# Cross-attention plus mixture-of-experts block: the second layer of the last pair but one in two parts, other buffers and another order of fetches behind the pairs

## The reference

```
x = x + tanh(g_xattn[0]) * xattn(layernorm(x), ctx)      # 16 heads of 64, 64 context rows
x = x + tanh(g_ffn[0])   * ffn(layernorm(x))
ffn:   shared = (sum over 2 shared experts of gelu(x @ sw1 + sb1) @ sw2 + sb2) / 2
       gates  = x @ router_w + router_b;  top 2 of 8 experts, softmax over the two
       moe    = sum over the two chosen of prob * (gelu(x @ w1[e] + b1[e]) @ w2[e] + b2[e])
       return shared + moe
```

## Time and profile before

| what | us |
|---|---|
| three runs: median (lowest to highest) | 379.96 (378.42 to 380.06) |
| the profiled execution's own time | 378.79 |
| span of its trace | 377.1 |
| PE busy | 368.1 |
| DVE busy | 280.7 |
| ACT busy | 239.9 |
| POOL busy | 219.8 |

### The profile page before, as it was taken

The page is one execution under the profiler, slowest core; times in us unless marked ns, Lnnn a source line. Parts: engine busy times, 40 slices in busy tenths (PEclk is TensorE's granted clock), DMA queues, the critical chain, the costliest instruction groups (busy, mean ns, idle before and its releaser), DMA issues.

```text
span 377.1 us, 8869 instructions
## 1 busy us (share of the span) xinstructions
PE 368.1 (98%) x2805; PEld 349.8 (93%) x2806; DVE 280.7 (74%) x612; ACT 239.9 (64%) x538; POOL 219.8 (58%) x268
## 2 busy tenths in 40 slices
PE   8999999999999999999999999999999998999996
PEld 7987989999999899899999989999999997889995
DVE  5799898888988997799899887555655554554486
ACT  2675456556656635787878857666666665677740
POOL 6558775788788762477782245556565654653200
PEclk9999999999999999999999999999999999999999
DMA  7990000000000066502930112213222324650397
GB/s 219 292 350 20 2 30 15 16 27 30 14 14 28 17 241 248 237 4 35 303 115 3 29 44 86 72 56 95 75 87 81 93 79 127 199 138 29 108 352 253
DMA packets 33855, 40.15 MB, mean 106 GB/s; under 512 B 9690, under 2 KB 26524, under 8 KB 33692
## 3 DMA queue, kind: packets, MB, share of 16 engines
q1 hardware_dynamic: 28976, 29.40, 25.3%
q0 software_dynamic: 4768, 10.28, 8.9%
q10 hardware_dynamic: 76, 0.02, 0.0%
HBM read 27.88 MB, written 11.68 MB: 105 GB/s over the span
## 4 chain that ended last, share of the span: by engine, by line
PE 79%; DMA 6%; DVE 5%; issue 3%; ACT 3%; POOL 3%; DVEq 0%; ACTq 0%; POOLq 0%
PE psum L1385 11%; PE psum L1362 11%; PE psum L1278 10%; PE psum L1322 10%; PE psum L1619 8%; PE psum L1525 7%; PE psum L1499 5%; PE psum L1580 4%; DMA y_rows<-ybuf 4%; PE psum L1238 3%; DMA xsl<-y_rows,table 2%; PE psum L1512 1%; PE psum L1604 1%; PE psum L1136 1%; PE psum L1310 1%
## 5 line engine op out<-in xcount | busy, mean ns | idle before, releaser
L762 POOL DMA_INDIRECT y_tok<-ysl,table x39 | 38.9, 997 | 42.0 <-ACT ysl L1047 37.1
L755 POOL DMA_INDIRECT xsl<-y_rows,table x39 | 39.3, 1008 | 32.1 <-PE psum L1385 11.8
L728 POOL DMA_INDIRECT names<-named,pos x32 | 35.2, 1099 | 12.8 <-issue 8.2
L683 POOL TENSOR_TENSOR Eb<-Eb,rinv 128x512 f32<-128x512 f32 x32 | 33.5, 1065 | 11.6 <-DVE rinv L1833 11.6
L1091 ACT ACTIVATE hr<-psum,b_cur 128x256 f32<-128x256 f32 x48 | 20.1, 471 | 22.1 <-DVE b_cur L2128 12.3
L924 ACT ACTIVATE yTb<-psum 128x256 f32<-128x256 f32 x16 | 6.2, 384 | 42.6 <-PE psum L1342 42.6
L1619 PE MATMUL psum<-xsT_hi,w_cur 128*128 128x256 f32 x192 | 31.0, 284 | 0.0
L663 POOL TENSOR_TENSOR half_sum<-Eb 128x512 f32<-128x512 f32 x16 | 20.7, 1292 | 11.5 <-ACT Eb L879 11.3
L2177 DVE TENSOR_TENSOR hr_lo<-hr,hr_hi 128x512 fp32r<-128x512 f32 x24 | 16.6, 693 | 13.3 <-ACT hr_hi L1104 13.0
L1619 PEld LDWEIGHTS psum<-xsT_hi,w_cur 128*128 128x128 f32 x192 | 26.5, 192 | 0.0
L1047 ACT ACTIVATE ysl<-psum,table 128x256 f32<-128x256 f32 x39 | 17.1, 466 | 12.8 <-PE psum L1499 8.7
(11 more groups left out here) (275 smaller groups left out, 1247.6 us busy)
## 6 DMA issues: line engine op xcount, KB each, us to landing
w_raw<-in_L_ffn_w SPq DMA_DIRECT2D x2, 4096.0 KB, 16.8
y_got<-y_tok SPq DMA_DIRECT2D x8, 512.0 KB, 7.6
sw_raw<-in_L_ffn_sw SPq DMA_DIRECT2D x2, 1024.0 KB, 12.3
y_rows<-ybuf SPq DMA_DIRECT2D x16, 128.0 KB, 1.7
sw_lo_kept<-sw_lo SPq DMA_DIRECT2D x1, 2048.0 KB, 8.7
sw_lo<-sw_lo_kept SPq DMA_DIRECT2D x8, 256.0 KB, 3.5
xs_all<-in_x SPq DMA_DIRECT2D x3, 512.0 KB, 13.8
out<-xs_all SPq DMA_DIRECT2D x3, 512.0 KB, 3.1
```

The lines of the kernel that those rows point to most:

```text
L683: nc.gpsimd.tensor_tensor(Eb[q][:, heads, :], Eb[q][:, heads, :], rinv[:, q, heads].unsqueeze(2).broadcast_to([P, H // 2, CTX]), ALU.mult) ...
L728: nc.gpsimd.indirect_dma_start(names, bass.IndirectOffsetOnAxis(ap=pos[:, k, t:t + 1], axis=0), named[:, k, t, :], None).then_inc(scattere ...
L755: nc.gpsimd.indirect_dma_start(into[:, s % 2, :], None, y_rows, bass.IndirectOffsetOnAxis(ap=table[:, s, 0:1].bitcast(I32), axis=0)).then_ ...
L762: nc.gpsimd.indirect_dma_start(y_tok, bass.IndirectOffsetOnAxis(ap=table[:, s, 1:2].bitcast(I32), axis=0), ysl[:, s % 2, :], None).then_in ...
```

## The change

- PE: the second layer of 26/27 is made in two parts, h = 0 in `double(11)` where all of it stood, h = 1 in `step(30)` behind the transposes of 31.
- Tile 30's rows are gathered into `xsl2` instead of `xsl`; the waits of gathers 30 to 32 and of the later transposes are renumbered to fit.
- POOL: gather 31 moves from d = 9 (behind gather 30) to d = 10 (behind scatters 24 and 25, ahead of gather 32). Gather 34 moves ahead of scatter 28. The order is now: scatter 22, 23, gather 30; scatter 24, 25, gather 31, 32; scatter 26, 27; gather 33, 34; scatter 28, 29; gather 35; scatter 30; gather 36 and so on.
- ACT, in d = 11: the high part of tile 31's rows is taken ahead of `kept(1)`.
- DVE: `half_left(1)` of the pair 28/29 moves into `step(30)`, behind the low part of tile 31's rows; `bias_weights` moves from d = 10 to `step(33)`, behind `hidden_left(32)`.

```diff
@@ gather
-                elif 1 <= d < DOUBLES:
+                elif 1 <= d < DOUBLES or s == SINGLE1:
                     pool.wait_ge(xt_psum, s - 3)
+                elif SINGLE1 < s < SINGLE1 + 3:
+                    pool.wait_ge(xt_psum, SINGLE1)
                 elif s >= 2:
                     pool.wait_ge(xt_psum, s - 1)
-                into, loaded = (xsl3, xsl2_loaded) if d == 0 else (xsl2, xsl2_loaded) if wide(d) else (xsl, xsl_loaded)
+                second = wide(d) or s == SINGLE1
+                into, loaded = (xsl3, xsl2_loaded) if d == 0 else (xsl2, xsl2_loaded) if second else (xsl, xsl_loaded)
@@ POOL's order
-                    if d + 3 == DOUBLES:
-                        gather(SINGLE1 + n)
+                if d + 3 == DOUBLES:
+                    gather(SINGLE1)
                 if d + 2 == DOUBLES:
+                    gather(SINGLE1 + 1)
                     gather(SINGLE1 + 2)
-            for s in range(SINGLE1 + 1, SLOT_TILES):
-                if s + 2 < SLOT_TILES:
-                    gather(s + 2)
+            gather(SINGLE1 + 3)
+            gather(SINGLE1 + 4)
+            scatter(SINGLE1 - 2)
+            for s in range(SINGLE1 + 2, SLOT_TILES):
                 scatter(s - 3)
+                if s + 3 < SLOT_TILES:
+                    gather(s + 3)
@@ ACT, double
-                kept(1)
                 if d == DOUBLES - 1:
                     turned(SINGLE1 + 1, 1)
+                kept(1)
@@ PE, turn
-                pe.wait_ge(xsl_loaded[par], 16 * (s // 2 + 1) if s < DOUBLE0 else 16 * (s // 2 + 1) - 16 * (DOUBLES // 2))
+                rows = xsl2 if s == SINGLE1 else xsl
+                if s == SINGLE1:
+                    pe.wait_ge(xsl2_loaded[0], 16 * (DOUBLES // 2 + 1))
+                elif s < DOUBLE0:
+                    pe.wait_ge(xsl_loaded[par], 16 * (s // 2 + 1))
+                else:
+                    pe.wait_ge(xsl_loaded[par], 16 * ((s + par) // 2 - DOUBLES // 2))
@@ PE, give_wide, step, double
-            def give_wide(s, n):
+            def give_wide(s, n, halves=range(2)):
...
-                for h in range(2):
+                for h in halves:
...
-                if s == SINGLE1 + 1:
+                if s == SINGLE1:
+                    give_wide(s - 4, 0, range(1, 2))
+                elif s == SINGLE1 + 1:
                     give_wide(s - 3, 1)
-                elif s >= 2 and s != SINGLE1:
+                elif s >= 2:
...
-                    give_wide(s - 2, 0)
+                    give_wide(s - 2, 0, range(1))
@@ DVE, step, double (half_left now takes the tile as well)
-                if s >= 1 and s != SINGLE1:
+                if s == SINGLE1:
+                    half_left(s - 2, 1)
+                elif s >= 1:
                     hidden_left(s - 1, 1 - par)
+                if s == SINGLE1 + 3:
+                    bias_weights(EARLY, LAST)
...
                 if d == DOUBLES - 1:
                     bias_and_hidden(SINGLE1, 0)
-                half_left(1)
+                else:
+                    half_left(s, 1)
                 if more:
                     move_weights(par, 1)
-                if d == DOUBLES - 2:
-                    bias_weights(EARLY, LAST)
```

More of the change, by code:

```diff
@@ L1487, in turn @@
                 for k in range(KD):
-                    last = nc.tensor.transpose(bank[par][:, k * P:(k + 1) * P], xsl[:, par, k * P:(k + 1) * P], ident[:, :])
+                    last = nc.tensor.transpose(bank[par][:, k * P:(k + 1) * P], rows[:, par, k * P:(k + 1) * P], ident[:, :])
                 last.then_inc(xt_psum, 1)
@@ L2170, in step, with half_left @@
                     columns_rest(EARLY, late)
+            def half_left(s, h):
+                dve.wait_ge(ht_hi, s + (h + 1))
+                nc.vector.tensor_tensor(hr2_lo[:, 2 * h:2 * h + 2, :], hr2[:, :, :], hr2_hi[:, 2 * h:2 * h + 2, :].bitcast(F32),
+                                        ALU.subtract).then_inc(ht_lo, 1)
             def double(d, par, s, j):
[L2174 to L2178, removed]
                 if d == 0:
@@ L2191, in double @@
                     turned_wide(s + 2, 1 - par)
-                half_left(0)
+                half_left(s, 0)
                 if more:
```

## The result

The changed kernel took 380.65 us (median of 11 runs, 379.71 to 381.96), the kernel before 379.02 us in the same session (11 runs, 377.73 to 380.06). The ratio is 1.0038 with a 95% interval of 1.0023 to 1.0053, that is 1.4 us slower (0.9 to 2.0). The forecast was 380.2 us, 0.7 above its base, with its likeliest case inside 0.5%.

The account below looks back on a forecast made before the run. PE, busy for 98% of the span, was taken as the bound. The terms 0.50 + 1.07 - 1.01 + 0.15 = +0.7 us on a base of 379.5 gave 380.2 us, range 378.2 to 382.2.

Parts of the forecast that it names:

- its base: Starting time of 379.5 us, set between the profiled execution's 378.79 and the three-run median 379.96.
- its likeliest case: Whole kernel: +0.7 us, giving 380.2 us, chance 0.57; no change was given 0.71.
- the deciding step: POOL fetching tile 31's rows one place later: PE stops from 313.06 to 314.94, first layer 31 +0.50 us.
- Halves of the second layer: PE, second layer 26/27 in two parts: 12 products take 1.44 us, first layer 30 starts about 311.68 instead of 313.26.
- The 0 for tile 30's low part: Before first layer 30: PE's wait for the low part of tile 30's rows, taken as 0, upper end 0.3 us.
- Gather 31: POOL slot at 312.10, landing 2.8 us, rows at 314.90; first layer 31 at 317.12 instead of 316.62, +0.50 us.
- Outputs and scatter 27, up to first layer 33: ACT and POOL: output 26 2.05 later, scatter 27 landing in 3.8, gelu 31 at 323.9; first layer 33 +1.07 us.
- Step 34: PE's wait for gather 35, landing at 331.1 with transposes due at 331.55, is gone: -1.01 us.
- `bias_weights` in step 33: DVE: 1.72 us of work delays `hs` of 34 to about 333.1; +0.15 us, bounds 0 and 1.0.
- Sum: Whole kernel: 0.50 + 1.07 - 1.01 + 0.15 = +0.7 us, put on 379.5 to give 380.2 us.
- the first term: Wait for tile 31's rows before first layer 31: +0.50 us; +0.3 with a 2.6 us landing, +1.5 with 3.8.
- "from both sides": Gather 30 on POOL keeps its place, more than 4 us before it is due: 0 either way.

## Why the prediction was right

The sign, the size within 1 us, and the deciding step held; one cause was overlooked and one small term missed. By the prediction's steps:

- *Halves of the second layer.* First layer 30 was to start 4.62 us behind first layer 28/29 (311.68); it did at 4.72, since the 12 products took 1.60 us (310.61 to 312.21) instead of 1.44. The 0 for tile 30's low part was right: gelu started at 310.14, where 311.39 was before.
- *Gather 31.* Slot expected at 312.10, which is 312.53 on the changed trace's clock; it was 312.45. Landing 2.8 taken, 3.1 measured, idle time 1.88 taken, 1.81 measured. First layer 31 came 0.74 later than before (10.30 against 9.56) instead of 0.50: the 0.3 of the landing. That this place on POOL decides is shown by putting it back: -2.7 us.
- *Outputs and scatter 27, up to first layer 33.* +1.07 expected, +0.89 measured (1.63 less the 0.74). Output 26 was to be 2.05 later and was 2.30 later, counted from first layer 28/29; scatter 27 landed in 3.6 (3.8 taken), and gelu 31 started at 324.37, the predicted 323.9 plus the 0.43 by which this trace runs late. But PE's recorded wait in that step is for gather 33, which I had listed as standing in the queue and never given a landing time: issued at 321.57, there at 324.8. The two waits end within 0.1 us of each other, so the size was right for a reason that was only half of it, and that is luck. The kernel with gather 33 early shows scatter 27's half by itself (0.51 us of idle time); with gather 33 early and the reload late neither is left, and step 32 takes 3.48 us.
- *Step 33.* I had no term for scatter 28's landing and output 30. It cost 0.41 us (3.89 instead of 3.48).
- *Step 34.* -1.01 expected, 3.50 instead of 4.49 measured: -0.99. Gather 35 took 3.8 us, not the 5.1 taken, but PE asked for it 1.8 us behind its landing, so this did not matter.
- *`bias_weights` in step 33.* +0.15 taken, 0.02 measured; `hs` of 34 was done at 333.78 and its transposes started at 334.12. In exchange the move is what lets the halves work at all, which the prediction used (gelu at 309.9) but did not price: 1.4 us, by the two kernels that differ in it with gather 31 early (0.9967 and 1.0003).
- *Sum.* +0.7 predicted, +1.05 in the trace (26.99 against 25.94), +1.4 (0.9 to 2.0) over the runs. The base of 379.5 was 0.5 above the 379.02 measured for the kernel before, which made up for about half of what the sum lacked: between the medians the change cost 1.6 us, and 380.2 lies 0.45 below the 380.65 measured. That 380.2 came so close is in part luck.

The prediction's sentence that gathers and scatters took 2.4 to 2.8 us without the reload and 3.8 to 5.5 beside it holds for the rows that it cites, and not for the whole of that trace: gathers 30 and 31, with the reload far behind them, took 4.0 and 3.1, and scatter 28, beside it, 3.6.

The Trainium skill's figure of 2.0 us plus bytes over the rate (page "DMA: Bandwidth & Descriptors", section "Anatomy of one DMA — SWDGE (gpsimd) path"), as an estimate 2.3 us for a gather, would have made the first term near 0; gather 31 took 3.1, and the least of 39 gathers in the changed kernel 2.7. The Trainium skill's rule that a completion lands only behind that DMA engine's earlier writes, those of other queues too, from the same page (section "Queues, rings and completion order"), agrees with the landings: scatters 26 and 27 took 4.2 and 3.8 beside the reload and 2.4 and 2.4 in all four kernels in which it came later. So would a plain sharing of the engines between the transfers, and no run here separates the two. Nor is being beside the reload enough for a long landing: in the changed kernel scatter 26, issued at 318.97 between pieces of it, took 2.5.

## What to carry to other kernels

When an edit makes the bound engine ask for something sooner, list every transfer that it asks for in the next steps with its issue slot and its landing, also those that the edit does not move; the gain ends at the first that is late. A queue that runs in program order is priced by its slots: a gather set one place back, behind two scatters that wait for a result, came 4.9 us later (307.6 to 312.5) and turned a gain of 1.3 us into a loss of 1.4. Idle slots of such a queue, here the one ahead of scatter 26, can take the next fetches: by itself that gave nothing clear of the noise (0.9958 against 0.9967), with the reload late it did (0.9942 against 0.9988).

## What the runs showed of the hardware

- *A landing can be long without the reload.* Gather 30 has the reload far behind it and took 3.7 to 4.6 us in all thirteen traces of the table, against a median of 2.8 for all gathers; where it took 4.5 or more, PE waited for it by 0.32 to 0.43 us. The prediction priced it at 0 "from both sides"; in the trace of the kernel before it landed 0.08 us before PE asked for it (305.86 plus 4.0, against 309.94). In all thirteen traces one load of instructions (queue 8, one packet of 0.02 MB) falls beside gather 30; in the kernel before none falls in 299 to 303.2, where gathers 28 and 29 took 2.7 and 2.6. Scatter 19, near 292.5 us and in the same place in every kernel, is a test that nobody planned: in six traces such a packet falls beside it, and there it took 3.8 to 4.4 us; in the other seven none does, and there it took 2.4 (six of them; the seventh, with `bias_weights` back, has no landing for it). It does not always lengthen a transfer: scatter 28 in the changed kernel with the reload late had one beside its end and took 2.6. That the load is the cause is likely by this, but no run moved it.
- *The clock.* After an idle time of 2.02 us the granted clock was 0.50 (1.2 GHz) for some 3 us, in the trace of the changed kernel with the reload late. After 1.81 us in the changed kernel's own trace it stayed at 1.00. Over the runs, a mean clock of 0.996 or less came up in 4 of 11 runs of the changed kernel and 5 of 12 of the one with the reload late, the two that idle about 2 us in step 30; elsewhere in one of the 91 runs of the kernel before that stood beside the experiments, and in none of the other kernels. The runs' times hardly separate by it: in the changed kernel the four have a median of 380.97 us and the other seven one of 380.42, which is still 1.4 above the kernel before. So the clock is not what makes the change a loss; how much of the 1.4 it adds stays open.
